# A graph layer on one core: half the ring of gathered rows, fourteen weight loads on another queue, one reduction moved back

## The reference

```
gates    = ssp(edge_state @ We1 + be1) @ We2 + be2
gates    = gates * (1 - sigmoid(5 * (distance - 3.5)))
h        = ssp(concat(x[src], x[dst]) @ Wn1 + bn1) @ Wn2 + bn2
sums     = zeros.at[dst].add(h * gates)
new      = x + ssp(sums @ Ws1 + bs1) @ Ws2 + bs2
out      = layernorm(x + new)
```

## Time and profile before

| | us |
|---|---|
| median of 3 runs | 2000.88 |
| lowest and highest | 2000.53, 2002.76 |
| the profiled execution's own time | 2002.99 |
| its span, first to last instruction | 2001.1 |
| POOL busy | 1485.6 (74%) |
| PE busy | 1730.7 (86%) |
| ACT busy | 1532.0 (77%) |
| DVE busy | 1285.7 (64%) |

### The profile page before, as it was taken

One profiled execution on the slowest core, in us unless ns is written; L12 is line 12 of the kernel. 1 busy time (PEld: TensorE's weight loads), 2 busy tenths in 40 slices (PEclk: granted clock), 3 DMA queues, 4 the chain that ended last, 5 costly groups with the idle time before them and its releaser, 6 DMA issues.

```text
span 2001.1 us, 53540 instructions
## 1 busy us (share of the span) xinstructions
PE 1730.7 (86%) x16249; PEld 1323.6 (66%) x16249; DVE 1285.7 (64%) x3512; ACT 1532.0 (77%) x3368; POOL 1485.6 (74%) x1572
## 2 busy tenths in 40 slices
PE   4699999888888888888889889888888988898887
PEld 3477777766666666666666666666666666666665
DVE  4578887666665655566656666666666666666665
ACT  2589998877777777777777877787878777787785
POOL 6777777777777777777777777777777777777772
PEclk7799999999899999999999999999999999999998
DMA  5433343333333333333333333333333333333331
GB/s 120 121 86 97 96 96 97 84 85 83 80 76 70 74 73 72 73 72 73 72 73 74 77 76 71 78 76 70 81 75 74 73 76 73 71 82 75 73 74 31
DMA packets 255904, 157.77 MB, mean 79 GB/s; under 512 B 44873, under 2 KB 226518, under 8 KB 255838
## 3 DMA queue, kind: packets, MB, share of 16 engines
q1 hardware_dynamic: 202124, 104.94, 18.0%
q0 software_dynamic: 50048, 51.35, 15.9%
q10 hardware_dynamic: 3666, 0.68, 0.2%
HBM read 146.94 MB, written 9.87 MB: 78 GB/s over the span
## 4 chain that ended last, share of the span: by engine, by line
POOL 59%; issue 22%; PE 11%; DVE 3%; SPq 2%; ACT 1%; DMA 1%; ACTq 1%; DVEq 1%; POOLq 0%
POOL ga L449 59%; PE ps L609 3%; PE ps L622 3%; PE ps L626 1%; SPq L331 1%; PE ps L571 1%; PE ps L561 1%; PE ps L639 1%; DVE hid L1076 1%; DMA ga<-in_x_dram,srcT 1%; DVE hid L1080 1%; PE ps L563 1%; DMA w_tab<-w_i 0%; SPq L326 0%; SPq L317 0%
## 5 line engine op out<-in xcount | busy, mean ns | idle before, releaser
L449 POOL DMA_INDIRECT ga<-in_x_dram,srcT x1564 | 1484.6, 949 | 481.3 <-issue 473.0
L826 ACT ACTIVATE lg<-ps,bn1c 128x512 f32<-128x512 f32 x391 | 268.5, 687 | 305.3 <-PE ps L571 272.8
L622 PE MATMUL ps<-wn,hid 128*128 128x64 f32 x3128 | 445.1, 287 | 19.2 <-DVE hid L1080 16.5
L1076 DVE SCALAR_TENSOR_TENSOR hid<-ps,neg_b,lg 128x512 f32<-128x512 f32 x391 | 292.9, 749 | 228.5 <-ACT lg L841 214.4
L622 PEld LDWEIGHTS ps<-wn,hid 128*128 128x128 f32 x3128 | 390.2, 196 | 51.2 <-DVE hid L1080 24.9
L561 PE MATMUL ps<-ident,ea 128*128 128x128 f32 x782 | 172.4, 303 | 216.8 <-DMA ga<-in_x_dram,srcT 147.8
L818 ACT COPY xe<-ps 128x512 f32<-128x512 f32 x391 | 229.9, 588 | 124.0 <-PE ps L563 109.0
L609 PE MATMUL ps<-xe,wn 64*128 64x256 f32 x1564 | 289.5, 449 | 0.0
L561 PEld LDWEIGHTS ps<-ident,ea 128*128 128x128 f32 x782 | 79.8, 143 | 301.5 <-issue 283.9
L626 PE MATMUL ps<-we,hid 128*128 128x128 f32 x1564 | 272.2, 299 | 0.0
L1114 DVE TENSOR_TENSOR acc<-acc,ps 64x64 f32 x782 | 168.2, 215 | 161.8 <-issue 155.3
(11 more groups left out here) (124 smaller groups left out, 1848.5 us busy)
## 6 DMA issues: line engine op xcount, KB each, us to landing
ea<-in_edge_attr_dram SPq DMA_DIRECT2D x195, 256.0 KB
ga<-in_x_dram,srcT POOLq DMA_INDIRECT x1564
bw<-b_tab SPq DMA_DIRECT2D x782, 32.0 KB
relb<-rel_tab SPq DMA_DIRECT2D x196, 64.0 KB
b_tab<-share SPq DMA_DIRECT2D x25, 250.0 KB
out_dram<-xs SPq DMA_DIRECT2D x25, 125.0 KB
xs<-in_x_dram SPq DMA_DIRECT2D x3, 750.0 KB
rows_i<-in_dst_dram SPq DMA_DIRECT2D x1, 768.0 KB
```

Source lines behind the costliest of these rows:

```text
L449: pool.indirect_dma_start(to[:, t % 2, t // 2, :], None, x, bass.IndirectOffsetOnAxis(ap=idx[:, t:t + 1], axis=0)).then_inc(done, 16)
L622: pe.matmul(hg[:, t * D:(t + 1) * D], hid[:, u % 2, t * P:(t + 1) * P], wn2[:, :], start=False, stop=False, skip_group_check=True)
L826: act.activation(lg[:, u % 2, 0:QUAD].rearrange("p (k e) -> p k e", k=2), z[:, :, 0:PAIR], ACT.Abs, bias=bn1c[:, 0:1]).then_inc(n_abs, 1)
L1076: dve.scalar_tensor_tensor(out=hid[:, u % 2, 0:QUAD].rearrange("p (k e) -> p k e", k=2), in0=ps[:, 2 * (u % 2):2 * (u % 2) + 2, 0:PAIR], s ...
```

## The change

ARING goes from 16 to 8 (so `ga` and its semaphores are halved, the wait of POOL begins at quad 8, POOL reads the flag after 8 quads, and PE's loops are unrolled over 8). Fourteen weight loads go from ACT's queue to SP's, behind SP's loads of src and ahead of its stores of the shares. On DVE the reduction to the greatest moves behind the subtraction, the casts and the copies of `xT`; it now reduces the destinations after the subtraction, so that one small operation falls away. The flag is read by PE only ahead of L548, no longer ahead of the shares. ACT copies the first two groups of `relT` before it stores `rel_tab`.

```diff
@@ -18,7 +18,7 @@
 QUAD = 2 * PAIR
 W = 64
 RING = 4
-ARING = 16
+ARING = 8
 EPS = 1e-5
 SHARES = 2
 BRING = 8
@@ -338,6 +338,23 @@
             load_tail(ed, rows_f[2], ld_dist)
             sp.dma_start(rows_i[:, 0, 1:RG - 1, :], head(src, 1, RG - 1)).then_inc(ld_src[1], 16)
             load_tail(src, rows_i[:, 0], ld_src[1])
+
+
+            sp.dma_start(wn2[:, :], Wn2).then_inc(ld_w, 16)
+            sp.dma_start(we2s[:, :], We2).then_inc(ld_w, 16)
+            sp.dma_start(bn1c[:, :], col(bn1)).then_inc(ld_w, 16)
+            for h in range(2):
+                half = slice(h * D, (h + 1) * D)
+                sp.dma_start(be1c[half, :], col(be1)).then_inc(ld_w, 16)
+                sp.dma_start(bs1c[half, :], col(bs1)).then_inc(ld_w, 16)
+                sp.dma_start(ws1[half, :], Ws1).then_inc(ld_w, 16)
+                if h == 0:
+                    sp.dma_start(ws2[half, :], Ws2).then_inc(ld_w, 16)
+            sp.dma_start(ws2[D:P, :], Ws2).then_inc(ld_b, 16)
+            for h, v in enumerate((bn2, be2)):
+                sp.dma_start(brow[:, h, :], row(v).broadcast_to([P, D])).then_inc(ld_b, 16)
+            sp.dma_start(bs2r[:, :], row(bs2).broadcast_to([P, D])).then_inc(ld_b, 16)
+
             def store_share(g, slot):
 
                 if isinstance(g, int) and g < SHARES:
@@ -512,17 +529,16 @@
 
             pe.wait_ge(src_rows, 1)
             transpose_rows(0, 0, 0)
-            pe.wait_ge(span_ready, 1)
-            pe.transpose(ps[0:1, 5, 0:P], spanmax[:, 0:1], ident[:, :]).then_inc(span_t, 1)
             pe.wait_ge(rel_rows, 1)
             for g in range(2):
                 transpose_rows(1, g, 1 + g)
             pe.wait_ge(ld_wn, 64)
-            pe.wait_ge(flag_ready, 1)
             for g in range(SHARES):
                 turn(g)
             for g in range(SHARES):
                 shares(g)
+            pe.wait_ge(span_ready, 1)
+            pe.transpose(ps[0:1, 5, 0:P], spanmax[:, 0:1], ident[:, :]).then_inc(span_t, 1)
             for g in range(2, RG):
                 transpose_rows(1, g, 1 + g)
 
@@ -543,6 +559,7 @@
             pe.matmul(ps[:, 7, 2 * D:3 * D], shift[0:D, 2, :], ws2[0:D, :], start=True, stop=True).then_inc(bias_mm, 1)
             pe.wait_ge(bias_ready, 1)
             pe.wait_ge(ld_bd, 16 * 4)
+            pe.wait_ge(flag_ready, 1)
 
             for hg in ps_hg:
                 mm = pe.matmul(hg, ident[:, :], bsum[:, :, :, :].rearrange("p h k d -> p (h k d)"), start=True, stop=True)
@@ -761,21 +778,6 @@
                 half = slice(h * D, (h + 1) * D)
                 act.dma_start(we1[half, :], We1).then_inc(ld_bd, 16)
                 act.dma_start(we2[half, half], We2).then_inc(ld_bd, 16)
-            act.dma_start(wn2[:, :], Wn2).then_inc(ld_w, 16)
...
-            act.dma_start(bs2r[:, :], row(bs2).broadcast_to([P, D])).then_inc(ld_b, 16)
-
             act.wait_ge(iotas, 2)
             act.copy(iota_n[:, :], iota_i[:, :]).then_inc(iota_f, 1)
             for h in range(2):
@@ -785,13 +787,13 @@
 
             act.wait_ge(w_ready, 1)
             act.dma_start(w_tab.rearrange("a (g p c) -> p (a g) c", p=P, c=2), w_i[:, :, :]).then_inc(w_stored, 16)
+            for g in range(2):
+                tv, pv = evacuate_rows(relT, g, 1 + g)
+                act.copy(tv, pv).then_inc(row_e, 1)
             act.wait_ge(rel_ready, 1)
             for k in range(2):
                 act.dma_start(rel_tab[k].rearrange("(g p) e -> p g e", p=P),
                               rel_u8[:, :, k * PAIR:(k + 1) * PAIR]).then_inc(rel_stored, 16)
-            for g in range(2):
-                tv, pv = evacuate_rows(relT, g, 1 + g)
-                act.copy(tv, pv).then_inc(row_e, 1)
             act.wait_ge(w_stored, 16)
             act.dma_start(w_all[:, :], w_tab[:, 0:NQ * 2]).then_inc(w_loaded, 16)
             for g in range(SHARES):
@@ -920,13 +922,13 @@
                     node_square(g)
                     node_root(g)
             with act.Else():
-                for s in range(ARING):
+                for s in range(2 * ARING):
                     if s == SHARE0 - 2:
                         act.wait_ge(ld_x[1], 16)
                     fast_step(s, s % RING, None, s % 4 if s >= 2 else None)
                 for n in range(2, NS):
                     act.wait_ge(ld_x[n], 16)
-                with act.Fori(ARING, SHARE1 - 7, 4) as s:
+                with act.Fori(2 * ARING, SHARE1 - 7, 4) as s:
                     for u in range(4):
                         fast_step(s + u, u, None, u)
                 for s in range(SHARE1 - 4, SHARE1):
@@ -986,18 +988,9 @@
             dve.wait_ge(ld_dst, 16 * N_DST)
             link(dve.tensor_copy(rows_f[1][:, :, :], rows_i[:, 1, :, :]))
             drows = rows_f[1][:, :, :].rearrange("p g (k e) -> p g k e", k=2)
-            dve.tensor_reduce(dmax[:, :, 0, :], drows, AX_X, ALU.max)
             link(dve.tensor_reduce(dmin[:, :, :], drows, AX_X, ALU.min))
             link(dve.tensor_scalar(dmin[:, :, :], dmin[:, :, :], float(N - W), None, ALU.min))
             dve.tensor_copy(w_i[:, :, :], dmin[:, :, :]).then_inc(w_ready, 1)
-
-            dve.tensor_tensor(dmax[:, :, 0, :], dmax[:, :, 0, :], dmin[:, :, :], ALU.subtract)
-            link(dve.tensor_tensor(dmax[:, :, 1, :], lim[:, :].unsqueeze(2).broadcast_to([P, RG, 2]), dmin[:, :, :],
-                                   ALU.subtract))
-            link(dve.tensor_tensor(dmax[:, :, 2, :], dmin[:, :, :], lim_b[:, :].unsqueeze(2).broadcast_to([P, RG, 2]),
-                                   ALU.subtract))
-            dve.tensor_reduce(spanmax[:, :], dmax[:, :, :, :].rearrange("p g s c -> p (g s c)"), AX_X,
-                              ALU.max).then_inc(span_ready, 1)
             dve.tensor_tensor(drows, drows, dmin[:, :, :].unsqueeze(3).broadcast_to([P, RG, 2, PAIR]),
                               ALU.subtract).then_inc(rel_rows, 1)
             dve.wait_ge(rel_rows, 1)
@@ -1005,17 +998,25 @@
                 ins = dve.tensor_copy(rel_u8[:, :, k * PAIR:(k + 1) * PAIR].rearrange("p g (j e) -> p g j e", j=2),
                                       rows_f[1][:, :, k * PAIR:(k + 1) * PAIR].rearrange("p g (e j) -> p g j e", j=2))
             ins.then_inc(rel_ready, 1)
-            dve.wait_ge(span_t, 1)
-            link(dve.tensor_reduce(flagf[0:1, 0:1], ps[0:1, 5, 0:P], AX_X, ALU.max))
-            dve.tensor_scalar(flag_i[0:1, 0:1], flagf[0:1, 0:1], W - 0.5, None, ALU.is_gt).then_inc(flag_ready, 1)
 
             for g in range(SHARES):
                 dve.wait_ge(t_mm, g + 1)
                 dve.tensor_copy(xT[:, g, :, :], ps_t[g].rearrange("p (h n) -> p h n", h=2)).then_inc(t_e, 1)
+
+
+            dve.tensor_reduce(dmax[:, :, 0, :], drows, AX_X, ALU.max)
+            dve.tensor_tensor(dmax[:, :, 1, :], lim[:, :].unsqueeze(2).broadcast_to([P, RG, 2]), dmin[:, :, :], ALU.subtract)
+            link(dve.tensor_tensor(dmax[:, :, 2, :], dmin[:, :, :], lim_b[:, :].unsqueeze(2).broadcast_to([P, RG, 2]),
+                                   ALU.subtract))
+            dve.tensor_reduce(spanmax[:, :], dmax[:, :, :, :].rearrange("p g s c -> p (g s c)"), AX_X,
+                              ALU.max).then_inc(span_ready, 1)
             for g in range(SHARES):
                 dve.wait_ge(sh_mm, g + 1)
                 dve.tensor_copy(share[0:PB, g, 1:4:2, :],
                                 ps_sh[g][:, 1, :].rearrange("p (h f) -> p h f", h=2)).then_inc(sh_dve, 1)
+            dve.wait_ge(span_t, 1)
+            link(dve.tensor_reduce(flagf[0:1, 0:1], ps[0:1, 5, 0:P], AX_X, ALU.max))
+            dve.tensor_scalar(flag_i[0:1, 0:1], flagf[0:1, 0:1], W - 0.5, None, ALU.is_gt).then_inc(flag_ready, 1)
 
             dve.wait_ge(ld_src[1], 16 * 4)
             dve.tensor_copy(rows_f[0][:, 1:RG - 1, :], rows_i[:, 0, 1:RG - 1, :])
```

## The result

The changed kernel takes 2004.79 us (median of 19 runs, 2001.86 to 2006.56), the kernel before in the same sessions 2001.34 us (19 runs, 1999.45 to 2003.71). The medians are 3.4 us apart. The ratio is 1.0014, with a 95% interval of 1.0008 to 1.0020, which is 2.8 us (1.6 to 4.0). So the change costs about 3 us, less than the 0.2% that one measurement can tell from no change, but it is there over 19 runs. The forecast was 2003.6, 2.7 us more than before.

The account below looks back on a forecast made before the run. POOL's gathers were taken to bound the kernel from start to end. The ring's 9.5 us less the front part's 6.8 left a 2.7 us stall, added to 2000.88 for 2003.6 us, 0.13% slower; range 2000.5 to 2008.5.

Parts of the forecast that it names:

- What bounds the kernel: Whole run: POOL's gathers set the time, as head 6.7, pace 1960.0, any stall of POOL and tail 34.4 us.
- The ring's price: POOL at quads 16 and 17: with PE's old times, waiting for places in the ring of 8 costs 9.5 us.
- there is room before quad 16: Ring of 8 in the start-up: quad 8 is gathered at 47 to 49 us, quad 0 turned at 46.11, so no wait.
- d: Front part up to quad 9: how much earlier it comes, 6.8 us, taken off the ring's 9.5 us.
- the stretch from quad 0 to quad 9: PE's turning, 56.7 us: taken as unchanged and moved as a whole, give or take 2 us.
- the column bound: Front part: the greatest's column, not `w_tab`'s branch, decides when the distances' turning starts, 22.0 us instead of 28.80.
- POOL's starts don't move: POOL's first gather hangs on the first copy of `srcT` alone, ahead of everything changed, so its starts stay.
- the rule of the ring: SP's queue: by the skill's rule of ring order, the shares' stores queue behind the fourteen loads; the forecast sum stayed.
- the loads are hidden on SP: SP's queue: the fourteen loads end at 19.1, before the shares' stores at 20.3, with 1.2 us to spare.
- Front part gains too little: Rival: POOL waits at quads 16 and 17 and keeps the loss, 2006.4 to 2010.4 us; chance 0.25.
- No stall: Rival: x's load stretch shortens by 2.7 us or d exceeds 9.5, giving 2000.9 us; chance 0.08.
- The faster one: Rival: POOL's gathers run at a quicker pace and the time is 1994.2 us; chance 0.04.

Follow-up runs that it names:

- e1: The changed kernel with the ring back at 16 quads and nothing else changed; 2006.91 us beside 2005.55 on that chip, ratio 1.0006.
- e2: The kernel before with the ring of 8 alone, its front part as before; ratio 1.0036.
- e6: The kernel before with the ring of 8 and the fourteen weight loads on SP's queue, both reductions still ahead; ratio 1.0020.
- e5: The changed kernel, ring of 8, with its fourteen weight loads back on ACT's queue; ratio 1.0043.
- e4: The changed kernel, ring of 8, with the four late loads of x spread between quads instead of issued in a row; 2006.62 us, ratio 1.0002.
- e9 to e12: The changed kernel, e6, and twice e2 with e4's edit, in later sessions where the kernel before was 26% to 27% slower; ratios 0.9885, 0.9901, 0.9897, 0.9906.
- e8: e4 with e7's eight subtractions and quad 0's indices loaded straight to their places by ACT's queue; 1998.81 us beside 2001.60, ratio 0.9986.
- e7: e1 with DVE's one subtraction of two tensors made eight operations of one tensor and a column; ratio 0.9995.

## Why the prediction was right

**What bounds the kernel.** Right. POOL's pace, head and tail made the time in every run of the first sessions; e1 takes the front part's whole gain and returns none. The last gather, forecast for 1969.4, came at 1968.05, by the gathers' pace and not by the stall.

**The ring's price, 9.5 us with the old front part.** Right in size: e2's trace has 9.4. Wrong in one detail, the sentence that there is room before quad 16: it looked at quad 8 alone. In the trace of before quad 6 is turned at 81.91 and POOL begins quad 14 at 78.59, and e2's first pause is ahead of quad 14. Since the latest quad sets the whole loss, the sum isn't touched.

**d, the front part's gain.** The term 6.8 came out at 6.3 for quad 9 (102.77 to 96.46). By the rule the loss is then 9.5 - 6.3 = 3.2 us, and that is what the trace has at quad 17 (93.56 to 96.74). Of these 3.2 us only 2.2 are pauses, because POOL itself came 1.0 us later to quad 16. That d came so near is in part luck. Its two halves were both off and nearly cancel: the front part gained 7.6 us and not 6.8 (the distances' turning began at 21.11, forecast 22.0; 0.5 us of that is DVE, which had the column ready at 19.02 instead of 19.55), and the stretch from quad 0 to quad 9 took 57.9 us instead of 56.7. I had moved it as a whole. The order of the steps was right: ACT had its half of the shares done at 19.20 and began the third group of `relT` at 19.86, so the column bound, by 0.7 us.

**"POOL's starts don't move."** The step that failed. One gather takes 2.94 us where the longest so early had taken 1.93; this is the latter, in the trace of the kernel before:

```profile
15.05 1.93 POOL L449 DMA_INDIRECT ga<-in_x_dram,srcT  x1 [0.30 <-issue]
```

It began 1.2 us into DVE's subtraction, the changed kernel's 0.2 us into it, and both ended 0.85 us after it. So POOL is 0.8 us behind from quad 2 on. With the ring of 8 the wait ahead of quad 17 swallows that, and the forecast isn't touched; with the ring of 16 it is seen: e1 is 0.5 us behind at quad 18, with a gather of 1.99 us.

**The edits and d.** The prediction follows both edits in one chain and gives no share to either; the expectation of e6 did, 4.5 us to the loads and the rest to the reduction, and was wrong. By e5 and e6 the loads give all of it: without them quad 9 stays at 102.1, with them alone it is at 95.2.

**SP and the rule of the ring.** Right that the loads are hidden on SP. The last of the fourteen is issued at 18.08 + 0.43 and the stores of the shares go at 19.45, 1 us later (forecast 19.1 and 20.3), `relb` at 27.80 (28.6):

```profile
18.08 0.43 SPq L356 DMA_DIRECT2D bs2r<-in_L_gnn_bs_dram  x1
19.45 0.69 SPq L365 DMA_DIRECT2D b_tab<-share  x2
27.80 0.65 SPq L317 DMA_DIRECT2D relb<-rel_tab  x1
```

The prediction read the 8.3 us from the stores to `relb` as their landing. It is more than that: SP waits for several landings and then goes on by itself for some 1.8 us. Its waits, in the kernel before (first line), the changed kernel (next two) and e1 (last two):

```profile
SPq L271 <- DMA b_tab<-share: 5.8, 1, 5.8
SPq L271 <- DMA b_tab<-share: 4.3, 1, 4.3
SPq L378 <- DMA w_all<-w_tab: 1.5, 1, 1.5
SPq L271 <- DMA b_tab<-share: 4.9, 1, 4.9
SPq L378 <- DMA w_all<-w_tab: 3.2, 1, 3.2
```

The waits add up to 5.8 us in the kernel before and in the changed one, and to 8.1 us in e1, which has the same front part. The landings in the traces of the first sessions say when the second store was complete. With the fourteen loads on ACT's queue (before, e2, e5) it took 6.1 us from its issue. With the loads on SP's queue it took 6.1 us in the changed kernel and 6.9 to 8.4 us in the six others. That the stores can be late behind the loads is what the Trainium skill's rule says ("DMA: Bandwidth & Descriptors", "Queues, rings and completion order"); six of seven traces are in line with it. They don't show that the order in SP's ring is the reason: `w_all`, which ACT issues, is late too (it landed 1.4 us after its issue before, 3.6 us in the changed kernel and 4.9 us in e1). Nor does it cost anything here: in e1 `relb` goes 2.0 us later than in the changed kernel, and quad 0 is turned 0.5 us earlier.

**The rivals.** "Front part gains too little" is what e2 and e5 are, at 7 to 9 us. "No stall" is e4. The faster one, by POOL's pace, didn't come: the mean stayed 949 ns.

## What to carry to other kernels

Where one engine runs at a steady pace from start to end and the others are quicker in the steady part (not so in e9 to e12), a smaller ring is paid for once: by the worst of "when is the place free" against "when would it be used", and that is found in the start-up, not in the steady part. Hold the two timelines against each other quad by quad before choosing a depth. Work that makes the other engines start earlier is worth only what it takes off that wait; beyond that, look at the pacing engine's own first start (e8), and at the burst of transfers that makes one early step late (e4).

## What was not expected of the hardware

A gather that POOL issued while DVE subtracted two tensors of SBUF (2.29 us, 10.85 to 13.14) took 2.94 us and ended 0.85 us after that subtraction; with the same work as eight operations of one tensor and a column it took 0.96 us (e7). A gather that began 0.05 us ahead of the subtraction took its usual 0.94 us (kernel before, 13.80). This agrees with the Trainium skill, "SBUF — State Buffer", "Who interferes with whom", by which a DVE instruction with two SBUF inputs contends with a GpSimd instruction that reads SBUF. The same section reports that such an operation did not stall a transfer issued by GpSimd, and infers that it leaves the making of descriptors alone; for these gathers the measured 2.94 us says otherwise, and it decides.

A cast seems to do it too, though no run took the cast away. A gather beside a cast of 1.23 us took 1.98 us in e8. In the other kernels that cast lies beside POOL's first gather (6.90 to 8.13 in the changed kernel, the gather from 6.48 to 8.24): it took 1.60 to 2.13 us in all the others of the first sessions, and 1.11 us in e8, where the cast comes later.

PE's granted clock takes part of what an earlier start is worth: eight turnings cost 1.20 us at 1.00 and 1.95 us at the half level. From the start of the distances' turning to that of the source rows' it is 4.29 us in e7 and 4.83 us in the changed kernel, with the same order of work. Quad 9 didn't move with it: it is turned at 96.5 in both.
